# A two-layer sequence model on one core: dt's softplus moved out of PSUM, its sum to GpSimd, and four edits of order

## The chip, the core and the metric

One NeuronCore of a Trainium2 chip runs the whole program. It has TensorE (PE, matmul), VectorE (DVE), ScalarE (ACT), GpSimd (POOL) and the queue of SyncE (SP) that issues most transfers. The metric is the device time of one execution in microseconds; the time before is the median of three executions.

## What is computed

The input x is 4 x 1024 tokens of 256 values, all in float32. The first layer is a state-space block, the second a mixture of experts:

```python
# layer 1, on n = layernorm(x)
xc, z  = split(n @ W_in.T)                       # 256 + 256 columns
xs     = silu(conv3(xc, conv_w))                 # along the tokens
dt_param, Bp, Cp = split(xs @ W_x.T)             # 64, 16, 16
dt     = softplus(dt_param @ W_dt.T + b_dt) + 1e-5
s_t    = exp(-exp(A_log) * dt_t) * s_(t-1) + Bp_t * dt_t * xs_t   # 16 states a channel
y      = (Cp @ W_C.T) * sum_over_states(s) + D_param * xs
x      = x + layernorm((y @ W_out.T) * silu(z))
# layer 2, on n = layernorm(x): 8 experts, 2 for each token, and a shared one
out    = sum over the token's 2 experts e of weight_e * (gelu(n @ W1[e] + b1[e]) @ W2[e] + b2[e])
out   += gelu(n @ sW1 + sb1) @ sW2 + sb2
x      = x + layernorm(out)
```

## The kernel before

**Tiles.** The 4096 tokens are cut into NC = 8 chunks of TC = 512. Layer 1 holds the channels on the 128 partitions in two halves (c = 0, 1) and the chunk's 512 tokens along the free axis. Each chunk needs 32 scans: k = 0 to 31 counts 16 states times two halves. For each state TensorE spreads one row of Bp over the partitions (`spread`, L1007), VectorE multiplies it by u = dt * xs (`mult`, L1274) and runs the recurrence (`scan`, L1299), ScalarE makes the factors A = exp(nea * dt) (`decay`, L1587), and GpSimd adds the finished state to the sum of states (`scan` on its side, L1717, tile Ssum).

**The order.** Nothing schedules at run time. `timetable()` runs once in Python and writes one list of steps, PLAN; every engine walks that list and issues its own part of each step, so an engine's instructions stand in the list's order and a waiting instruction holds up all that stand behind it on that engine. The clock of the list is the scan: `main(i)` yields once per scan k of chunk i, and beside it run generators that are advanced by a share of their steps at each k:

- `prep(i + 1)`: layer norm, transpose (`xT`, L948), x and z projections (`xc`, L962; `z`, L976), convolution, silu, `dbc`, and dt of the next chunk, advanced by `prepare(k)` between FIRST_PREP = -3 and LAST_PREP = 27.
- `post(i - 1)`: of the chunk before, the product with C (`cmat`, L1012; `ymul`, L1305), the out projection, the gate, two layer norms (`stats` and `normal` of kinds 2 and 3, with `residual`, L1725, between), the stores, the transpose `nT` (L1035) and the gate's logits.
- `route(r)`: in three rounds, the top 2 and the tables that sort tokens by expert (`table`, L1736, GpSimd's indirect transfers).
- `pairs()`: groups of 256 tokens through the second layer, two at a time. A group is 8 `up` matmul pairs in four steps (L1077 for the shared expert, L1088 for a routed one), one `gelu` over both groups' hidden values (L1643, with a load of the activation table ahead of it and behind it), four `down` steps (L1121), and for a routed group a `gather` (L1747) ahead and a `scatter` (L1767) behind, both indirect transfers issued by GpSimd. In the last chunks `calls` = 58 steps of it are taken in each chunk.

Steps that fall due later stand in `agenda` and are written out by `tick()`, which also asks `fetch()` for the next gather and weights.

**PSUM.** Of 8 banks, 3 belong to the scan and NGEN = 5 go round among all other steps. A step in TAKING takes a bank, one in GIVING gives it back. `room()` lets a group's matmul take one only while at most NGEN - 3 are open.

**dt.** For chunks 1 to 7 ScalarE writes relu(p + b) from the bank into dts (L1563) and |p + b| back into the bank (L1567), then exp(-|.|) and ln(1 + .) in place in the bank (L1572, L1575). VectorE adds the bank, 1e-5 and dts into dts (`dt_sum`, L1262), which gives the bank back. GpSimd multiplies dts by xs into us (L926).

**The end.** When the last scan is done, all 8 banks are free for groups, `direct()` runs the remaining groups back to back, and `finishing()` does the last layer norm and the result chunk by chunk.

## Time and profile before

| | |
|---|---|
| runs of the kernel before | 1190.28, 1192.75, 1194.93 us; median 1192.75 |
| the profiled execution's own time | 1200.83 us |
| its span, first to last instruction | 1199.0 us |
| mean granted TensorE clock | 0.898 |
| busy, share of the span | PE 85%, PEld 68%, DVE 55%, ACT 54%, POOL 57% |
| chain that ended last, by engine | PE 54%, POOL 18%, issue 11%, DVE 8%, ACT 7%, DMA 1% |
| largest lines of that chain | L1121 22%, L1088 12%, L1717 9%, L1077 7%, L1100 6%, L1299 4%, L1736 3% |
| L1717 GpSimd's adds | x240, 303.1 us busy, 1287 ns mean |
| L1299 VectorE's scans | 148.3 + 141.2 us (x120 each) |
| L1747, L1767 gathers and scatters | x71 each, 70.2 and 112.5 us on POOL |

A view by stretches is read as follows: the preamble ends and the first scan starts at 35.5 us; the eight chunks' first scans start at 35.5, 97.4, 162.5, 232.5, 311.5, 389.6, 473.8 and 562.5 us; the last scan ends at about 654 us; from about 744 us to 1189 us TensorE runs groups alone; the last 10 us hold the final layer norm of the last 256 tokens and the last stores. Idle time of an engine is put to the instruction in front of which it passed, with what released it.

### The profile page before, as it was taken

The page shows a single profiled execution, that of the slowest core. Times are in us where ns is not written, and L with a number is a line of the kernel's source. Part 1 is how long each engine was busy: PE and PEld are TensorE (multiplying, and loading weights), DVE is VectorE, ACT ScalarE, POOL GpSimd, SP SyncE. Part 2 cuts the span into 40 slices and gives each one's busy share as a digit, 9 for nine tenths or more (in the row PEclk, how much of TensorE's full clock was granted, in tenths as well). Part 3 has the DMA queues.
Part 4 walks back from the last instruction along what each step waited for, and adds up shares of the span by engine and source line. Part 5 has one row for each costly group of instructions (what it writes and reads, how often), then busy time and mean ns, then how long its engine had stood idle before and what let it go on. Part 6 is the DMA issues. An engine that isn't in the chain of part 4 may idle for free.

```text
span 1199.0 us, 15407 instructions
## 1 busy us (share of the span) xinstructions
PE 1020.7 (85%) x4654; PEld 820.6 (68%) x4654; DVE 662.3 (55%) x1158; ACT 642.4 (54%) x1238; POOL 684.7 (57%) x666
## 2 busy tenths in 40 slices
PE   5437497878978879988949897999999999999996
PEld 3213175656656557766737775889999999998885
DVE  6899999998988898878955350010011000010333
ACT  5776869778587686886652531233333333333342
POOL 0687967769489997799774446432433333322211
PEclk9667587877968898999979997999999999999998
DMA  8210010202002016144463582598999988863511
GB/s 286 63 36 1 35 36 18 71 1 88 1 18 71 1 53 212 37 137 111 104 169 109 163 272 52 146 297 249 349 313 309 303 278 269 275 180 62 175 63 53
DMA packets 141635, 163.91 MB, mean 137 GB/s; under 512 B 26344, under 2 KB 126976, under 8 KB 141536
## 3 DMA queue, kind: packets, MB, share of 16 engines
q1 hardware_dynamic: 125872, 144.20, 37.1%
q0 software_dynamic: 15680, 18.72, 8.0%
q8 instruction: 37, 0.61, 0.2%
q14 instruction: 46, 0.38, 0.1%
HBM read 136.57 MB, written 26.74 MB: 136 GB/s over the span
## 4 chain that ended last, share of the span: by engine, by line
PE 54%; POOL 18%; issue 11%; DVE 8%; ACT 7%; DMA 1%; SPq 0%; DVEq 0%; POOLq 0%; ACTq 0%
PE psum L1121 22%; PE psum L1088 12%; POOL Ssum L1717 9%; PE psum L1077 7%; PE psum L1100 6%; DVE S L1299 4%; POOL list_d L1736 3%; ACT A L1587 2%; DVE psum L1274 1%; PE psum L962 1%; PE psum L1043 1%; PE psum L1064 1%; POOL scale L1661 1%; POOL gb L1725 1%; POOL acc_d L1767 1%
## 5 line engine op out<-in xcount | busy, mean ns | idle before, releaser
L1717 POOL TENSOR_TENSOR Ssum<-Ssum,S 128x512 f32<-128x512 f32 x240 | 303.1, 1287 | 73.4 <-DVE S L1299 72.5
L1121 PE MATMUL psum<-w,hT 128*128 128x256 f32 x1136 | 255.0, 382 | 8.5 <-issue 7.0
L1767 POOL DMA_INDIRECT acc_d<-y,ID x71 | 112.5, 1584 | 243.0 <-DMA acc_d<-y,ID 121.4
L1121 PEld LDWEIGHTS psum<-w,hT 128*128 128x128 f32 x1136 | 215.1, 192 | 38.3 <-issue 7.8
L1587 ACT ACTIVATE A<-dts,nea 128x512 f32<-128x512 f32 x256 | 175.2, 718 | 54.2 <-DVE S L1299 40.8
L1088 PE MATMUL psum<-XT,w 128*128 128x256 f32 x800 | 188.3, 390 | 15.2 <-issue 10.9
L1088 PEld LDWEIGHTS psum<-XT,w 128*128 128x128 f32 x800 | 154.4, 195 | 46.6 <-issue 17.7
L1274 DVE TENSOR_TENSOR psum<-us,psum 128x512 f32<-128x512 f32 x256 | 163.2, 683 | 35.6 <-PE psum L1007 35.4
L1299 DVE TENSOR_TENSOR_SCAN S<-A,carry,psum 128x512 f32<-128x512 f32 x120 | 148.3, 1266 | 0.2 <-issue 0.2
L1299 DVE TENSOR_TENSOR_SCAN S<-A,psum 128x512 f32<-128x512 f32 x120 | 141.2, 1205 | 3.3 <-POOL Ssum L1717 2.9
L1626 ACT ACTIVATE hT<-psum,bb 128x256 f32<-128x256 f32 x200 | 83.7, 471 | 105.0 <-PE psum L1088 71.7
L1077 PE MATMUL psum<-nT,s 128*128 128x256 f32 x512 | 134.3, 419 | 0.2 <-DVE nb L1312 0.2
L1431 DVE TENSOR_TENSOR psum<-bb,psum 128x256 f32<-128x256 f32 x71 | 26.9, 423 | 192.8 <-PE psum L1121 180.8
L1637 ACT ACTIVATE y<-psum,ID 128x256 f32<-128x256 f32 x71 | 29.8, 471 | 187.8 <-DVE psum L1431 180.5
L1121 PE MATMUL psum<-s,hT 128*128 128x256 f32 x512 | 127.5, 403 | 2.9 <-ACT hT L1643 2.9
L1421 DVE COPY XT<-psum 128x512 f32<-128x512 f32 x35 | 24.2, 691 | 188.3 <-PE psum L1064 155.5
L1077 PEld LDWEIGHTS psum<-nT,s 128*128 128x128 f32 x512 | 109.2, 214 | 21.7 <-issue 2.3
L1121 PEld LDWEIGHTS psum<-s,hT 128*128 128x128 f32 x512 | 104.3, 205 | 28.6 <-issue 12.9
L1007 PE MATMUL psum<-bst,SEL 96*128 96x512 bf16 x128 | 57.8, 453 | 71.8 <-DVE S L1299 66.5
L1747 POOL DMA_INDIRECT G<-xn_d,ID x71 | 70.2, 989 | 32.3 <-issue 18.5
L1007 PEld LDWEIGHTS psum<-bst,SEL 96*128 96x128 bf16 x128 | 14.2, 111 | 100.8 <-DVE S L1299 82.9
L1626 ACT ACTIVATE hT<-psum,sb1t 128x256 f32<-128x256 f32 x128 | 53.1, 469 | 50.4 <-PE psum L1077 50.2
(165 smaller groups left out, 1277.1 us busy)
## 6 DMA issues: line engine op xcount, KB each, us to landing
w<-W SPq DMA_DIRECT2D x92, 1024.0 KB
bb<-b SPq DMA_DIRECT2D x46, 128.0 KB
xnb<-x SPq DMA_DIRECT2D x16, 256.0 KB, 3.0
Xr<-x SPq DMA_DIRECT2D x16, 256.0 KB
x_d<-gb SPq DMA_DIRECT2D x8, 512.0 KB
xn_d<-nb SPq DMA_DIRECT2D x8, 512.0 KB
X<-x_d SPq DMA_DIRECT2D x16, 256.0 KB, 8.8
ACC<-acc_d SPq DMA_DIRECT2D x16, 256.0 KB, 5.4
```

What stands on the lines that cost most here:

```text
L1007: eng.matmul(BB[m % 2], SEL[:, n:n + 1].to_broadcast([96, 128]), bst[i % 2], start=True, stop=True).then_inc(spread, 1)
L1077: t = eng.matmul(ps[:, 256 * f:256 * f + 256], s1[:, k, 128 * (2 * u + f):128 * (2 * u + f) + 128], nT[i % 3][:, k, 256 * q:256 * q + 256] ...
L1088: t = eng.matmul(ps[:, 256 * f:256 * f + 256], w1[SLOT["w1", unit]][:, k, 128 * (2 * u + f):128 * (2 * u + f) + 128], XT[at % 2][:, k, :], ...
L1100: t = eng.matmul(ps[:, 128 * f:128 * f + 128], w1[SLOT["w1", unit]][:, k, 128 * (f0 + f):128 * (f0 + f) + 128], XT[at % 2][:, k, 128 * hal ...
L1121: t = eng.matmul(bank(g)[:, 256 * k:256 * k + 256], hT[n % 2][:, f, 128 * k:128 * k + 128], w[:, f, :], start=f == 0, stop=f == 7)
L1274: eng.tensor_tensor(bb if c else UB, us[i % 2][:, c, :], bb, ALU.mult).then_inc(mult, 1)
L1299: eng.tensor_tensor_scan(to, A[m % NA], BB[(m // 2) % 2] if c else UB, first, ALU.mult, ALU.add).then_inc(scan, 1)
L1587: eng.activation(A[m % NA], dts[i % 2][:, c, :], ACT.Exp, scale=nea[:, c, n:n + 1]).then_inc(decay, 1)
L1626: t = eng.activation(hT[n % 2][:, 2 * u + f, :], ps[:, 256 * f:256 * f + 256], fn, bias=bias[:, 2 * u + f:2 * u + f + 1])
L1717: eng.tensor_tensor(to, to, of, ALU.add).then_inc(nsum, 1)
L1747: eng.indirect_dma_start(G[n % 2][:, k, :], None, xn_d[0:TC * ROUND_END[r], :], bass.IndirectOffsetOnAxis(ap=ID[:, col, 0:1].bitcast(u32), ...
L1767: eng.indirect_dma_start(acc_d, bass.IndirectOffsetOnAxis(ap=ID[:, col, 1:2].bitcast(u32), axis=0), y[n % NY][:, k, :], None, compute_op=A ...
```

## The change

Six things are altered; the first is the title's, the others are of order.

1. **dt.** For all chunks |p + b| is written to us in SBUF, exp and ln work there in place, and the bank is given back at `dt_out`. For chunks 1 to 7 ScalarE adds 1e-5 in one more pass for each half (Identity with a bias), and GpSimd adds dts and us into dts; VectorE keeps the sum for chunk 0 only. `room()` now lets a group take a bank while at most NGEN - 2 are open.
2. **quiet.** While the two late layer norms of a chunk are under way, new gathers and due scatters are held back; `stats` of kind 2 and of kind 3 stand one scan later.
3. **The first chunk.** prep(1) is advanced from k = 0 on rather than from a start of -3.
4. **calls** goes from 58 to 54.
5. **The last chunk's final norm** is done in two halves (`last_stats`, `last_normal`, `last_result`).
6. **keep_busy.** TensorE multiplies zeros, 11 matmuls of 128x256 ahead of the first transposes and 3 ahead of the first projection.

```diff
     def tick():
 
         now[0] += 1
-        due = [row for at, row in agenda if at <= now[0]]
-        agenda[:] = [(at, row) for at, row in agenda if at > now[0]]
+        held = [item for item in agenda if item[0] > now[0] or quiet[0] and item[1][0] == "scatter"]
+        due = [row for at, row in agenda if (at, row) not in held]
+        agenda[:] = held
...
-        while len(open_uses) > room_for[0] - (2 if past[0] else 3):
+        while len(open_uses) > room_for[0] - 2:
             yield
...
         say("gated", i, 0, w0)
+        quiet[0] = not late
         yield
         say("gated", i, 1, w1)
-        yield from normalised(2, i, late)
+        yield
+        say("stats", 2, i)
+        quiet[0] = False
+        yield
+        yield
+        say("normal", 2, i, late)
+        quiet[0] = not late
+        yield
+        yield
         say("residual", i, late)
+        quiet[0] = False
         yield
         if not late:
             yield
             yield
+            quiet[0] = True
+            yield
             yield
         say("store_x1", i, late)
-        yield from normalised(3, i, late)
+        say("stats", 3, i)
+        quiet[0] = False
+        yield
+        yield
+        say("normal", 3, i, late)
+        yield
+        yield
...
-        if n < min(listed[0], turned[0] + 2):
+        if n < min(listed[0], turned[0] + 2) and not quiet[0]:
             say("gather", n)
...
-    def prepare(k):
+    def prepare(i, k):
 
         nonlocal done_prep
-        want = min(n_prep, -(-n_prep * (k + 1 - FIRST_PREP) // (LAST_PREP + 1 - FIRST_PREP)))
+        first = FIRST_PREP if i else 0
+        want = min(n_prep, -(-n_prep * (k + 1 - first) // (LAST_PREP + 1 - first)))
...
-                calls = 58 if listed[0] else 26
+                calls = 54 if listed[0] else 26
...
+    say("last_stats", 0)
+    yield
+    say("normal", 4, NC - 2, False)
+    say("result", NC - 2)
+    say("last_normal", 0)
+    say("last_result", 0)
+    yield
+    say("last_stats", 1)
+    say("last_normal", 1)
+    say("last_result", 1)
...
+            def keep_busy(ps, of, n):
+
+
+                for _ in range(n):
+                    eng.matmul(ps[:, 0:256], of[:, 0:128], of, start=True, stop=True)
...
-                    eng.activation(ps, ps, ACT.Abs, bias=bdt[:, c:c + 1]).then_inc(dt_out, 1)
+
+                    eng.activation(us[i % 2][:, c, :], ps, ACT.Abs, bias=bdt[:, c:c + 1]).then_inc(dt_out, 1)
                 elif step == "softplus":
-                    i, *gs = a
-                    for c in range(2):
+                    i, = a
+                    first = 6 * i - 2 if i else 0
+                    halves = [us[i % 2][:, c, :] for c in range(2)]
+                    for c, h in enumerate(halves):
                         eng.wait_ge(dt_out, 4 * i + 2 * c if i else c + 1)
-                        eng.activation(bank(gs[c]), bank(gs[c]), ACT.Exp, scale=-1.0).then_inc(softp, 1)
-                    for c in range(2):
-                        eng.wait_ge(softp, 4 * i + c + 1)
-                        eng.activation(bank(gs[c]), bank(gs[c]), ACT.Ln, bias=1.0).then_inc(softp, 1)
+                        eng.activation(h, h, ACT.Exp, scale=-1.0).then_inc(softp, 1)
+                    for c, h in enumerate(halves):
+                        eng.wait_ge(softp, first + c + 1)
+                        eng.activation(h, h, ACT.Ln, bias=1.0).then_inc(softp, 1)
+                    if i:
+                        for c, h in enumerate(halves):
+                            eng.wait_ge(softp, first + c + 3)
+                            eng.activation(h, h, ACT.Identity, bias=eps).then_inc(softp, 1)
...
+                elif step == "dt_sum":
+                    i, c = a
+                    if i:
+                        eng.wait_ge(softp, 6 * i + 3 + c)
+                        eng.tensor_tensor(dts[i % 2][:, c, :], dts[i % 2][:, c, :], us[i % 2][:, c, :], ALU.add).then_inc(dt_done, 1)
```

**TensorE, the start of the scans in chunk 0** (bst, SEL: spread; C, xnb: transposes of chunk 1; xnT, wxz: its projections). Before:

```order
L1007 MATMUL psum<-bst_131,SEL 128x512 x2
L948 MATMUL psum<-C,xnb 128x128 x8
L1007 MATMUL psum<-bst_131,SEL 128x512
L962 MATMUL psum<-xnT,wxz 128x512 x2
L1007 MATMUL psum<-bst_131,SEL 128x512
```

With the change:

```order
L1050 MATMUL psum<-bst_131,SEL 128x512 x3
L989 MATMUL psum<-C,xnb 128x128 x8
L1050 MATMUL psum<-bst_131,SEL 128x512
L1005 MATMUL psum<-xnT,wxz 128x512 x2
L1050 MATMUL psum<-bst_131,SEL 128x512
```

One more spread, that of state 2, stands ahead of the eight transposes; from there on each spread has moved one piece of chunk 1's preparation forward.

**ScalarE in chunk 2, around the gelu of the first pair of groups** (hT: hidden values; A: decays; edge, xs, zs: silu of the next chunk; gb: the layer norm of kind 2). Before:

```order
L1643 ACTIVATE hT_102<-hT_102 128x2048
L1463 ACT_TABLE_LOAD
L1587 ACTIVATE A_134<-dts_123,nea 128x512
L1527 ACTIVATE xs_122<-edge,xs_122,cw 128x1
L1530 ACT_TABLE_LOAD
L1530 ACTIVATE xs_122<-xs_122 128x512
L1527 ACTIVATE xs_122<-edge,xs_122,cw 128x1
L1530 ACTIVATE xs_122<-xs_122 128x512
L1534 ACTIVATE zs_128<-zs_128 128x1024
L1463 ACT_TABLE_LOAD
L1587 ACTIVATE A_135<-dts_123,nea 128x512
L1486 ACTIVATE gb<-gb,scale 128x256 x4
```

With the change:

```order
L1725 ACT_TABLE_LOAD
L1725 ACTIVATE hT_101<-hT_101 128x2048
L1725 ACTIVATE hT_102<-hT_102 128x2048
L1533 ACT_TABLE_LOAD
L1669 ACTIVATE A_139<-dts_123,nea 128x512
L1586 ACTIVATE xs_122<-psum,cw 128x512
L1586 ACTIVATE us_126<-psum,cw 128x512
L1586 ACTIVATE dts_124<-psum,cw 128x512
L1669 ACTIVATE A_140<-dts_123,nea 128x512
L1592 COPY zs_128<-psum 128x512
L1669 ACTIVATE A_141<-dts_123,nea 128x512
L1669 ACTIVATE A_142<-dts_123,nea 128x512
```

The gelu stood directly ahead of the silu and its two table loads, with the norm behind them; now it stands among the copies of the convolution's taps (xs, us, dts from psum), ten rows ahead of the silu. The same is found in chunks 3, 4 and 5.

**GpSimd in chunk 7, from the residual (gb) to the statistics of kind 3 (scale from mv30)**. Before:

```order
L1725 TENSOR_TENSOR gb_148<-Xr0_117,gb_148 128x512
L1725 TENSOR_TENSOR gb_148<-Xr1_118,gb_148 128x512
L1717 TENSOR_TENSOR Ssum11_146<-Ssum11_146,S_147 128x512
L1717 TENSOR_TENSOR Ssum10_145<-Ssum10_145,S_147 128x512
L1767 DMA acc_d<-y0_103,ID_69 4224x256 x2
L1717 TENSOR_TENSOR Ssum11_146<-Ssum11_146,S_147 128x512
L1717 TENSOR_TENSOR Ssum10_145<-Ssum10_145,S_147 128x512
L1767 DMA acc_d<-y1_104,ID_69 4224x256 x2
L1747 DMA G1_106<-xn_d,ID_69 128x256 x2
L1658 TENSOR_SCALAR scale_93<-mv30_89 128x4
L1659 TENSOR_SCALAR scale_93<-mv30_89 128x4
```

With the change:

```order
L1825 TENSOR_TENSOR gb_148<-Xr0_117,gb_148 128x512
L1825 TENSOR_TENSOR gb_148<-Xr1_118,gb_148 128x512
L1817 TENSOR_TENSOR Ssum11_146<-Ssum11_146,S_147 128x512
L1867 DMA acc_d<-y0_103,ID_69 4224x256 x2
L1867 DMA acc_d<-y1_104,ID_69 4224x256 x2
L1817 TENSOR_TENSOR Ssum10_145<-Ssum10_145,S_147 128x512
L1847 DMA G1_106<-xn_d,ID_69 128x256 x2
L1817 TENSOR_TENSOR Ssum11_146<-Ssum11_146,S_147 128x512
L1817 TENSOR_TENSOR Ssum10_145<-Ssum10_145,S_147 128x512
L1817 TENSOR_TENSOR Ssum11_146<-Ssum11_146,S_147 128x512
L1740 TENSOR_SCALAR scale_93<-mv30_89 128x4
L1741 TENSOR_SCALAR scale_93<-mv30_89 128x4
```

Both scatters (acc_d) and the gather (G1) still stand between the residual and the scale of kind 3, the two scatters now one behind the other; the adds (Ssum) that followed them stand behind, three of them right ahead of the scale.

## Rows read from the trace of the kernel before

**Rows 1.** Windows view: us; busy PE, PEld, DVE, ACT, POOL; PEclk; DMA share; GB/s
```profile
389.60:473.80 84.20, 68.83 (x282) 51.58 (x280) 73.02 (x120) 60.84 (x106) 75.70 (x72) 0.88 0.31 95
473.80:562.50 88.70, 79.40 (x345) 60.78 (x344) 72.79 (x119) 67.67 (x112) 73.86 (x76) 0.98 0.27 78
562.50:654.00 91.50, 72.40 (x326) 58.95 (x326) 67.64 (x96) 47.73 (x81) 62.67 (x58) 0.91 0.48 127
...
744.00:1189.00 445.00, 442.11 (x2403) 397.88 (x2403) 60.13 (x151) 150.37 (x409) 143.54 (x128) 0.99 0.73 222
```

**Rows 2.** Waits view, whole span: total us, times, longest us
```profile
DVE psum L1274 <- PE psum L1007: 35.4, 12, 13.0
...
POOL gb L1725 <- ACT gb L1486: 18.7, 4, 7.2
...
DVE stats L1181 <- POOL gb L1725: 11.6, 8, 3.5
...
DVE psum L1305 <- POOL Ssum L1717: 8.6, 3, 4.5
```

**Rows 3.** Timeline, preamble: start us, us, engine, line, [idle before <- releaser]
```profile
8.58 1.97 PE L948 MATMUL psum<-C,xnb 128*128 128x128 f32 x8 [8.58 <-ACT xnb L1486]
...
12.07 5.99 PE L962 MATMUL psum<-xnT,wxz 128*128 128x512 f32 x8 [1.22 <-ACT xnT L1497]
...
18.82 0.75 DVE L1232 SCALAR_TENSOR_TENSOR xs<-psum,cw,xs 128x511 f32<-128x511 f32 x1 [0.42 <-ACT xs L1510]
```

**Rows 4.** Timeline, first chunk, VectorE
```profile
44.95 1.29 DVE L1274 TENSOR_TENSOR psum<-us,psum 128x512 f32<-128x512 f32 x2 [3.69 <-PE psum L1007]
```

**Rows 5.** Tile and line views: count, ns min/median/max, first and last start us
```profile
L1262 DVE SCALAR_TENSOR_TENSOR dts<-psum,dts x16: 661/681/691, 30.0 to 547.0; 128x512 f32<-128x512 f32 x16
...
L926 POOL TENSOR_TENSOR us<-dts,xs x14: 1257/1264/1271, 88.5 to 552.8; 128x512 f32<-128x512 f32 x14
...
L1572 ACT ACTIVATE psum<-psum x16: 536/572/579, 28.4 to 539.3; 128x512 f32<-128x512 f32 x16
...
L1530 ACT ACTIVATE xs<-xs x16: 629/630/631, 19.5 to 502.7; 128x512 f32<-128x512 f32 x16
```

**Rows 6.** Timeline, chunk 2: ScalarE's gelu, VectorE's second statistics
```profile
185.83 3.71 ACT L1643 ACTIVATE hT<-hT 128x2048 f32<-128x2048 f32 x2
...
200.07 0.75 DVE L1181 BATCH_NORM_STATS2 stats<-gb 128x6 f32<-128x256 f32 x2 [2.38 <-POOL gb L1725]
```

**Rows 7.** Timeline, end of chunk 4: dt's sum, u on GpSimd, the next mult
```profile
378.52 1.28 DVE L1262 SCALAR_TENSOR_TENSOR dts<-psum,dts 128x512 f32<-128x512 f32 x2
...
386.44 2.49 POOL L926 TENSOR_TENSOR us<-dts,xs 128x512 f32<-128x512 f32 x2
...
388.39 1.29 DVE L1274 TENSOR_TENSOR psum<-us,psum 128x512 f32<-128x512 f32 x2 [0.62 <-PE psum L1007]
```

**Rows 8.** Timeline, chunk 6, TensorE and VectorE
```profile
527.66 2.71 PE L1121 MATMUL psum<-s,hT 128*128 128x256 f32 x8 [2.92 <-ACT hT L1643]
...
535.89 1.29 DVE L1274 TENSOR_TENSOR psum<-us,psum 128x512 f32<-128x512 f32 x2 [5.76 <-PE psum L1007]
```

**Rows 9.** Timeline, chunk 7: GpSimd, ScalarE and VectorE
```profile
610.87 1.55 POOL L1767 DMA_INDIRECT acc_d<-y,ID  x1 [2.42 <-DMA acc_d<-y,ID]
...
618.86 2.08 ACT L1486 ACTIVATE nb<-gb,scale 128x256 f32<-128x256 f32 x4 [9.65 <-POOL scale L1663]
...
629.19 1.29 DVE L1274 TENSOR_TENSOR psum<-us,psum 128x512 f32<-128x512 f32 x2 [13.04 <-PE psum L1007]
...
637.79 1.29 DVE L1274 TENSOR_TENSOR psum<-us,psum 128x512 f32<-128x512 f32 x2 [4.96 <-PE psum L1007]
```

**Rows 10.** Timeline, the end of the span, GpSimd and VectorE
```profile
1189.50 1.40 DVE L1181 BATCH_NORM_STATS2 stats<-ACC 128x6 f32<-128x256 f32 x4
...
1191.39 0.58 POOL L1658 TENSOR_SCALAR scale<-mv 128x4 f32<-128x4 f32 x1 [18.89 <-DVE mv L1187]
...
1194.54 1.28 DVE L1458 TENSOR_TENSOR X<-X,ACC 128x512 f32<-128x512 f32 x2
```

More of the change, by code:

```diff
@@ L88, in timetable @@
     now, room_for, listed = [0], [NGEN], [0]
+    quiet = [False]
     def say(*row):
@@ L207, in prep @@
             say("stats_x", 6)
-        for c, t in enumerate((t0, t1)):
-            say("dt_sum", i, c, t)
+        for c in range(2):
+            say("dt_sum", i, c)
             say("u", i, c)
@@ L553, in timetable @@
         chunk, whole = divmod(done, 2)
-        if n >= 2 and n % 2 and (whole or chunk < LATE or ("s", chunk, 1) in summed):
+        if n >= 2 and n % 2 and (whole or chunk < LATE or ("s", chunk, int(chunk < NC - 1)) in summed):
             part(final, 1)
@@ L563, in finishing @@
 def finishing(say):
-    for i in range(NC):
+    for i in range(NC - 1):
         say("stats", 4, i)
@@ L941, in _ @@
                     ps = take(g)
+                    if i == c == 0:
+                        eng.wait_ge(zeroed, 1)
+                        keep_busy(ps, G[0][:, 0, :], 11)
                     if c == 0:
@@ L959, in _ @@
                         eng.wait_ge(got_cw, 32)
+                    if i == c == 0:
+                        keep_busy(ps, G[0][:, 0, :], 3)
                     eng.wait_ge(xT_out, 2 * i + 2)
@@ L1200, in _ @@
                         read = edge_mv, 2
+                elif step == "last_stats":
+                    q, = a
+                    n = 2 * NC - 2 + q
+                    wait_whole(eng, NTH["s", NC - 1, q])
+                    eng.wait_ge(*read)
+                    for j in (2 * q, 2 * q + 1):
+                        i = eng.bn_stats(stats[:, j, :], of(4, NC - 1, j))
+                    i.then_inc(statd4, 1)
+                    eng.wait_ge(statd4, 2 * q + 1)
+                    if q == 0:
+                        eng.wait_ge(nmd[4], NC - 2)
+                    for j in (2 * q, 2 * q + 1):
+                        i = eng.bn_aggr(mv[4][(NC - 1) % 2][:, j, :], stats[:, j, :])
+                    i.then_inc(statd4, 1)
+                    read = statd4, 2 * q + 2
+                elif step == "last_normal":
+                    q, = a
+                    j = 2 * q + 1
+                    eng.wait_ge(nmd4, q + 1)
+                    eng.tensor_scalar(into(4, NC - 1, j), of(4, NC - 1, j), rs[4][(NC - 1) % 2][:, j:j + 1],
+                                      nm[4][(NC - 1) % 2][:, j:j + 1], ALU.mult, ALU.add).then_inc(normv[4], 1)
+                elif step == "last_result":
+                    q, = a
+                    n = 2 * NC - 2 + q
+                    eng.wait_ge(norma[4], 4 * (NC - 1) + q + 1)
+                    eng.wait_ge(normv[4], q + 1)
+                    eng.wait_ge(got_l[NC - 1], 32)
+                    eng.tensor_tensor(X1[n], X1[n], ACC[n], ALU.add).then_inc(resd, 1)
                 elif step == "stats_x":
@@ L1491, in _ @@
                         eng.preload_act_table_set("silu_and_others")
+                elif step == "last_normal":
+                    q, = a
+                    of, n = ACC[2 * NC - 2 + q][:, 0, :], (NC - 1) % 2
+                    eng.wait_ge(nmd4, q + 1)
+                    eng.activation(of, of, ACT.Identity, bias=nm[4][n][:, 2 * q:2 * q + 1],
+                                   scale=rs[4][n][:, 2 * q:2 * q + 1]).then_inc(norma[4], 1)
                 elif step == "xT_out":
@@ L1889, in _ @@
                         eng.dma_start(rows8(out[i // 2])[:, 2 * (n % 4):2 * (n % 4) + 2, :], X1[n]).then_inc(st_out[n % 4], 16)
+                elif step == "last_result":
+                    q, = a
+                    n = 2 * NC - 2 + q
+                    eng.wait_ge(resd, n + 1)
+                    eng.dma_start(rows8(out[NB - 1])[:, 2 * (n % 4):2 * (n % 4) + 2, :], X1[n]).then_inc(st_out[n % 4], 16)
             for k in range(4):
```

44 lines of the change are left out of this document (27 added, 17 removed).

## The prediction

> **What bounds the kernel now.** I first read the windows by stretch [rows 1]. From 744 us to 1189 us TensorE is busy 442.1 of 445.0 us: whatever is left when the scans end is worked off at a fixed pace, and nothing can be won there except work taken out of it. The order of the changed kernel takes none out: up to the last scan both plans hold 68 `up` and 64 `down` steps and 8 transposed groups. So the time moves by what the stretch of the scans, the preamble and the last ten microseconds lose, and by that alone.
>
> In the chunks VectorE is the busiest engine at first. Chunk 5 has GpSimd at 75.7 of 84.2 us against VectorE's 73.0, not counting what it loses between its own indirect transfers, so it is all but full; in chunks 6 and 7 no engine is full (TensorE 79.4 of 88.7, then 72.4 of 91.5), so these are chunks of waits [rows 1]. The waits view says which [rows 2]: VectorE stood 35.4 us for spreads, 12 times, the longest 13.0; 11.6 us for the residual by GpSimd, which itself stood 18.7 us for ScalarE's norm; and 8.6 us for the last adds of the states.
>
> **The change part by part**, against the profiled execution of 1200.8 us.
>
> *Preamble.* The first projections take 5.99 us for 8 records, most at the lower of TensorE's two clocks, and ScalarE's copy of the second ends 0.42 us after VectorE is free for it [rows 3]. VectorE is otherwise dense there, so warm matmuls can bring 0.5 us. Against it: 22 records of zeros stand ahead of the transposes. At the price of the slow projections (0.75 us a record of 512 columns, so 0.37 for 256) they take 8.2 us, and the last three matmuls, 6 records, 2.2 us, where TensorE had 8.58 us and then 1.22 us free [rows 3]. Bounds: 3 us lost, 1 us won; I take 0.5 won, since that gap and the faster projections behind it pay for the three.
>
> *First chunk.* The spread of state 2 stands behind the transposes of chunk 1, which wait for their input, and keeps VectorE for 3.69 us [rows 4]. It now stands ahead of them, and each later one has one piece of preparation fewer ahead. VectorE does one pair of scans more by the same time, 3.4 us (mult 1.29, the pair of scans 2.3, overlaps taken off). The two smaller waits behind it stay in part. Bounds 2 and 5.7.
>
> *dt's sum.* VectorE loses 2 x 0.68 us, 1.3 with the overlap, in each of chunks 0 to 6. GpSimd gains two adds at the price of its product u, 2 x 1.26 = 2.5 us [rows 5]. ScalarE gains two passes of 0.63 (the in-place silu in SBUF), 1.3 us. Exp and ln in SBUF rather than PSUM are four passes; in place in PSUM one took 0.57, the silu in SBUF 0.63 [rows 5], so 0.2 us more. ScalarE was busy 60.8 and 67.7 us in chunks 5 and 6 [rows 1] and has no queue that reaches the next chunk, so I charge it nothing; were that cover gone, it would cost 1.5 us a chunk.
>
> The Trainium skill says the same of the direction ("ScalarE: Activation LUTs", Step-by-step: what each stage is for): a write to PSUM is faster than one to SBUF. It speaks against this change; these rows put it at some 0.06 us a pass, and the sum is the same with or without it.
>
> Where GpSimd has room (chunks 0 to 3) VectorE's 1.3 us count in full: 5.2 us. In chunk 4 GpSimd reached u 7.9 us after VectorE had made dt (386.4 against 378.5), and VectorE then stood up to 4.5 us for the last add [rows 2, 7]. There the 2.5 us count, not the 1.3. The same holds for chunk 5.
>
> *Banks and the earlier gelu.* In chunk 2 the gelu (3.71 us and two table loads) stood ahead of silu and norm, the residual came behind the norm, and VectorE stood 2.38 us for its first half [rows 6]. Now it is ten rows earlier on ScalarE and the silu no longer stacks on it. Statistics of kind 3 also come one scan later. That removes nearly all of the 11.6 us [rows 2], but only where GpSimd does not bind: the eight waits lie in chunks 2 to 5, 2.9 us a chunk, and I count chunks 2 and 3, 5.8 us. In chunks 4 and 5 GpSimd's own waits for the norm go, some 5 us for both (18.7 in all, less the longest of 7.2 and one near it [rows 2]), less twice 2.5 for dt: nothing won. What is late next on ScalarE are the tap copies of the next chunk at scans 4 and 5; they have until scan 9, where the silu stands, so I cost them at nothing.
>
> *Holding back gathers and scatters* moves GpSimd's own work behind the norm's steps by one to three scans. Before chunk 5 there is none to hold, and later the group that needs a gather is two groups away, so I cost it at nothing; without that cover a transposed group would wait for it.
>
> *Chunk 6.* TensorE waited 2.92 us for the gelu (dt's second matmul and the spread stood behind it), and VectorE 5.76 us for that spread [rows 8]. The gelu comes one scan earlier, GpSimd has 2.5 us more, and four more `up` steps (6.9 us of TensorE) fall into this chunk, taken from the next. Bounds: 4 lost, 7 won; I take 2 won, near neither, because the extra matmuls eat most of the wait removed.
>
> *Chunk 7.* GpSimd waited for the first scatter's landing before it could issue the second (2.42 us), so the scale of kind 3 came late, ScalarE's norm waited 9.65 us, the gelu of two groups stood behind that norm, and TensorE's transposes and `down` steps held the spreads: 13.04 + 4.96 us of VectorE [rows 9]. In the new order both scatters and the gather still stand ahead of that scale, so GpSimd is as late as it was. But the gelu stands ahead of the norm now, so its 3.7 us and loads no longer come behind, and four `up` steps are gone from the chunk. Of 18 us I take 8 off; bounds 2 and 18.
>
> *The end.* Behind the last matmul stand a 0.69 us sum, statistics of four tiles, the scale on GpSimd, two norms and two results. Halved, the statistics save 0.7 of 1.40 and the results 0.6 of 1.28; aggregation and norm save 0.5 more by the same share. GpSimd's first step took 0.58 us against 0.24 elsewhere while VectorE added chunk 6's results [rows 10]; those now stand ahead of the last half, which saves 0.3 more on it and as much on the next step. 2.4 us.
>
> The Trainium skill has the reason ("SBUF — State Buffer", Who interferes with whom): a VectorE instruction with two SBUF inputs keeps GpSimd's reads out. The 0.58 us agree.
>
> **Sum:** 0.5 (preamble) + 3.4 (first chunk) + 5.2 (dt) + 5.8 (norm) + 2 + 8 (chunks 6, 7) + 2.4 (end) = 27.3 us. The profiled execution stood 8.1 us above the median of its runs; I take the same 27.3 off the median: 1192.75 - 27.3 = 1165.4.
>
> **The rivals.**
> 1. *GpSimd becomes the bound.* Its 2.5 us are paid in chunks 4 to 6, held-back scatters land on it in a heap, and chunk 7 keeps its 13 us wait. For: it is full in chunk 5, and the order of chunk 7. Against: 18.7 us of its waits are for the very norm that comes earlier. Gains in chunks 6 and 7 fall from 10 to 2 and chunks 4 and 5 cost 4: 27 - 8 - 4 = 15 won. 1178, from 1173 to 1184.
> 2. *The waits of chunks 6 and 7 go altogether.* They come from one queue that is late; once ScalarE is no longer stacked the lateness may not build. 7 + 18 instead of 10: 42 won, 1150.
> 3. *Nothing measurable, moved waits.* The gelu collides with the tap copies, the convolution comes late, and each chunk gives back at its `dbc` what it won. Left are the preamble, first chunk and end, 6 us, less GpSimd's price of 2.5: 1189.
> 4. *Slower: dt comes late at each boundary.* The decays of the next chunk now wait for GpSimd, in order behind its adds. At the end of chunk 4 GpSimd lagged 7.9 us; with its sums and u 13 us, where the next chunk's first mult came 9.9 us behind dt [rows 7]. That boundary would cost 3 us. From a lag of some 10 us at every boundary it decides: 7 boundaries at 5 us are 35, which is 8 more than the rest wins: 1200. Against: dt was last made at 547.0 [rows 5] and chunk 7's first scan came at 562.5, 15 us behind.
>
> **How the numbers follow.** A measurement of this kernel tells about 0.5%, 6 us, from no change. My forecast (20 to 36 us won) 0.56; rival 1 0.19; rival 2 0.13; rival 3 0.06; rival 4 0.06. Predicted 1165. The range leaves out rivals 3 and 4 and the ends of 1 and 2: 1151 to 1181. Faster 0.88, same 0.06, slower 0.06.
>
> **What would show it.** The first scans of chunk 2, 3 and 4 come earlier by some 6, 10 and 14 us than before; VectorE's waits for the residual are gone; u starts on GpSimd later behind VectorE's place than before, by 1.3 us; between 744 us and the end of the matmuls TensorE is as dense and as long. VectorE's waits for spreads fall from 35 us to about 20, the largest still in chunk 7. From the last matmul to the last instruction it takes 7.7 us rather than 10. I would be wrong in the step on chunk 7 if the longest wait is gone or whole, in the step on dt if ScalarE's decays stand for GpSimd's sum, and in the whole if the stretch of groups has grown by what the scans lost.

## The result and the profile after

| | before | changed |
|---|---|---|
| median of the runs | 1193.8 us (1190.28 to 1194.93, 4 runs) | 1205.49 us (1202.76 to 1206.2, 4 runs) |
| ratio, 95% interval | 1 | 1.0099 (1.0071 to 1.0126) |
| profiled execution: span, granted clock | 1199.0 us, 0.898 | 1203.6 us, 0.904 |
| last scan ends | 653.9 us | 655.1 us |
| last matmul ends | 1188.86 us | 1195.12 us |
| last matmul to end of the span | 10.1 us | 8.5 us |

The change costs about 12 us where I had forecast 27 won; the same kernel, run again on another chip (e13 below), gave a ratio of 1.0116. The two spans differ by only 4.6 us, since the profiled execution of before stood 8 us above its median; against the experiments below these 8 us lie behind the last scan.

First, the windows view of the changed kernel, a row for each of chunks 5, 6 and 7 and then the stretch of groups in four pieces (columns as in [rows 1]):

```profile
382.50:471.10 88.60, 65.45 (x282) 49.88 (x280) 71.69 (x118) 67.64 (x121) 77.79 (x74) 0.87 0.30 90
471.10:562.10 91.00, 80.73 (x362) 63.89 (x361) 71.58 (x118) 67.69 (x112) 72.93 (x74) 0.96 0.28 76
...
562.10:655.10 93.00, 74.22 (x315) 60.09 (x314) 68.19 (x97) 50.59 (x85) 67.57 (x62) 0.88 0.46 133
655.10:700.00 44.90, 39.96 (x166) 32.37 (x165) 13.08 (x35) 18.99 (x31) 21.47 (x23) 0.90 0.51 140
700.00:760.00 60.00, 59.11 (x301) 52.43 (x300) 17.46 (x70) 18.59 (x42) 34.36 (x33) 1.00 0.55 155
760.00:870.00 110.00, 93.38 (x525) 83.42 (x524) 10.16 (x21) 28.68 (x85) 38.63 (x32) 0.94 0.85 251
870.00:1195.10 325.10, 325.10 (x1769) 292.70 (x1767) 51.01 (x132) 113.72 (x306) 100.61 (x96) 1.00 0.71 220
```

The first scans of the chunks came at 35.2, 92.4, 160.7, 229.8, 305.8, 382.5, 471.1 and 562.1 us, where before they came at 35.5, 97.4, 162.5, 232.5, 311.5, 389.6, 473.8 and 562.5. So 5 us are won by chunk 1 and 7 in all by chunk 5; chunks 5 to 7 give everything back. I had forecast the first scans of chunks 2, 3 and 4 to come 6, 10 and 14 us earlier; they came 1.8, 2.7 and 5.7 us earlier. Then TensorE, which I had taken for fully fed, stands 16.6 of the 110 us from 760 us on. Before, from 744 us to the end, it stood 2.9 us [rows 1].

Waits view of the changed kernel (total, times, longest), for [rows 2]:

```profile
DVE psum L1348 <- PE psum L1050: 48.8, 21, 11.1
...
ACT A L1669 <- POOL dts L1794: 21.5, 10, 5.4
...
DVE psum L1379 <- PE psum L1055: 18.0, 5, 7.2
```

VectorE's 11.6 us for the residual are gone, as the change says. But its waits for spreads have grown from 35.4 to 48.8 us (I had forecast about 20), its wait for the matmul of C (`cmat`, L1055) from 2.6 to 18.0, and ScalarE stands 21.5 us for GpSimd's sum of dt, where before it stood 6.0 us for VectorE's. The end of chunk 4 shows how these hang together (timeline; ScalarE, GpSimd, TensorE, VectorE), at the place of [rows 7]:

```profile
373.15 0.19 ACT L1680 COPY lg<-psum 128x32 f32<-128x32 f32 x1 [3.24 <-PE psum L1086]
...
377.59 0.72 ACT L1669 ACTIVATE A<-dts,nea 128x512 f32<-128x512 f32 x1 [4.26 <-POOL dts L1794]
380.17 2.56 ACT L1669 ACTIVATE A<-dts,nea 128x512 f32<-128x512 f32 x4 [1.86 <-POOL dts L1794]
...
383.96 2.06 ACT L1556 ACTIVATE xnb<-xnb,scale 128x256 f32<-128x256 f32 x4
```
```profile
373.85 2.49 POOL L1817 TENSOR_TENSOR Ssum<-Ssum,S 128x512 f32<-128x512 f32 x2
376.30 1.26 POOL L1794 TENSOR_TENSOR dts<-dts,us 128x512 f32<-128x512 f32 x1
```
```profile
386.17 0.63 PE L989 MATMUL psum<-C,xnb 128*128 128x128 f32 x4 [3.20 <-ACT xnb L1556]
...
388.68 1.12 PE L1055 MATMUL psum<-dbc,wc 16*128 16x512 f32 x2
```
```profile
389.91 0.70 DVE L1379 TENSOR_TENSOR psum<-Ssum,psum 128x512 f32<-128x512 f32 x1 [4.98 <-PE psum L1055]
```

The operands of the sum were ready at 367.2 us (end of the Identity pass). GpSimd, in order behind its adds of the states, began it at 376.3. On ScalarE the decay of the next chunk (A) waits for it, and everything else stands behind that decay: the groups' copies and the norm of kind 1 (xnb). Behind that norm stand TensorE's transposes, behind these the spread and C's matmul, and VectorE loses 4.98 us.

And the stretch of groups, its fetches (SyncE) and TensorE's gap:

```profile
719.32 3.53 SPq L1966 DMA_DIRECT2D bb<-b  x1
763.05 0.38 SPq L1944 DMA_DIRECT2D ID<-list_d  x1
...
774.27 0.39 SPq L1962 DMA_DIRECT2D w<-W  x1
```
```profile
773.93 1.09 PE L1107 MATMUL psum<-C,G 128*128 128x128 f32 x4 [5.07 <-DMA G<-xn_d,ID]
783.26 9.10 PE L1131 MATMUL psum<-XT,w 128*128 128x256 f32 x32 [8.24 <-DMA bb<-b]
```

The last round's lists are read back from 763.05 us on (755.56 before). Behind them, in order on SyncE, the next weights are fetched at 774.27 (766.57 before), and TensorE stands for them until 783.26.

### The profile page after: what moved, and what is told of

Its sections match the earlier page's. It is cut to its first block, busy times and chain, and to the rows that moved or that the text cites. A ratio compares the mean times of both kernels' runs of the same rounds, so it can differ in the third digit from the quotient of the medians.

```text
span 1203.6 us, 15481 instructions
## 1 busy us (share of the span) xinstructions
PE 1006.0 (84%) x4682; PEld 817.5 (68%) x4682; DVE 654.3 (54%) x1145; ACT 648.9 (54%) x1252; POOL 703.6 (58%) x684
## 4 chain that ended last, share of the span: by engine, by line
PE 45%; POOL 17%; ACT 12%; issue 11%; DVE 5%; SPq 4%; DMA 3%; POOLq 0%; DVEq 0%; ACTq 0%
PE psum L1164 19%; PE psum L1131 8%; POOL Ssum L1817 8%; PE psum L1120 7%; PE psum L1143 5%; ACT A L1669 3%; POOL list_d L1836 3%; DVE S L1373 2%; ACT hT L1725 2%; DMA acc_d<-y,ID 2%; DMA bb<-b 1%; SPq L1942 1%; PE psum L1066 1%; ACT hT L1708 1%; PE psum L1086 1%
## 5 line engine op out<-in xcount | busy, mean ns | idle before, releaser
L1164 PE MATMUL psum<-w,hT 128*128 128x256 f32 x1136 | 257.9, 385 | 8.2 <-issue 6.5
L1131 PE MATMUL psum<-XT,w 128*128 128x256 f32 x800 | 184.4, 388 | 14.0 <-DMA bb<-b 8.2
L1348 DVE TENSOR_TENSOR psum<-us,psum 128x512 f32<-128x512 f32 x256 | 163.2, 683 | 49.1 <-PE psum L1050 48.8
L1120 PE MATMUL psum<-nT,s 128*128 128x256 f32 x512 | 126.5, 401 | 0.0
L1164 PE MATMUL psum<-s,hT 128*128 128x256 f32 x512 | 118.2, 383 | 1.2 <-ACT hT L1725 1.2
L1120 PEld LDWEIGHTS psum<-nT,s 128*128 128x128 f32 x512 | 103.5, 204 | 21.9 <-issue 5.0
L1164 PEld LDWEIGHTS psum<-s,hT 128*128 128x128 f32 x512 | 98.6, 193 | 21.4 <-issue 7.8
```

Of the source, the lines that this page charges most:

```text
L1120: t = eng.matmul(ps[:, 256 * f:256 * f + 256], s1[:, k, 128 * (2 * u + f):128 * (2 * u + f) + 128], nT[i % 3][:, k, 256 * q:256 * q + 256] ...
L1131: t = eng.matmul(ps[:, 256 * f:256 * f + 256], w1[SLOT["w1", unit]][:, k, 128 * (2 * u + f):128 * (2 * u + f) + 128], XT[at % 2][:, k, :], ...
L1164: t = eng.matmul(bank(g)[:, 256 * k:256 * k + 256], hT[n % 2][:, f, 128 * k:128 * k + 128], w[:, f, :], start=f == 0, stop=f == 7)
L1348: eng.tensor_tensor(bb if c else UB, us[i % 2][:, c, :], bb, ALU.mult).then_inc(mult, 1)
```

## The experiments

Four theories. **A**: the loss is the last routing round alone, late behind late logits. **B**: it is GpSimd's sum of dt; B1 by its place in GpSimd's order, B2 by its 2.5 us of work. **C** (formed after the first eight runs): the stretch behind the scans depends on where the last chunk's closing steps stand among the group steps (the `up` and `down` steps). "The stretch" is from the end of the last scan to the end of the last matmul. Each run was timed beside the kernel before; a ratio is to that, on its own chip. Edits are against the changed kernel and cut to what matters.

**e1: closing steps twice as fast behind the last scan.**
```diff
     for _ in beside:
         tick()
-        part(last, 1)
+        part(last, 2)
```


> The changed kernel with one edit: behind the last scan the last chunk's closing steps advance two, not one, per matmul step of the groups, so that its logits stand 10 group steps behind the last scan instead of 22 (15 in the kernel before). Theory A (the loss is the last routing round, which comes late behind logits moved off beat, so that TensorE has no group ready between 760 and 800 us): the gap there, about 14 us, goes, and the time is 1193 +-3, some 12 us less than the changed kernel's 1205.5. Theory B (the loss is GpSimd's sum of dt, which ScalarE's decays wait for in the chunks; the gap is only where the lateness shows): nothing is won or at most 4 us, 1201 to 1206.

1.0100 (1.0077 to 1.0123). The gap at 760 us shrank to 7.0 us, but TensorE now stood 10.8 us between 655 and 700 for the closing steps themselves; the stretch came to 536.5 us. Theory A in this form fell.

**e2: the sum on VectorE.**
```diff
-                    if i == 0:
-                        eng.wait_ge(softp, 3 + c)
-                        eng.scalar_tensor_tensor(dts[0][:, c, :], us[0][:, c, :], 1e-5, dts[0][:, c, :],
+                    eng.wait_ge(softp, 4 * i + 3 + c)
+                    eng.scalar_tensor_tensor(dts[i % 2][:, c, :], us[i % 2][:, c, :], 1e-5, dts[i % 2][:, c, :],
...
 ScalarE's Identity pass and GpSimd's sum are taken out
```


> The changed kernel with dt's sum made by VectorE from SBUF in all chunks, without ScalarE's Identity pass; order of steps untouched. Theory B: ScalarE's 21.5 us of waits for GpSimd's sum go, and with them a part of VectorE's 48.8 us for spreads; 5 to 10 us won, 1196 to 1200. Theory A: the order and its late logits are the same, the gap at 760 us stays at 12 us or more, and VectorE pays 1.3 us a chunk again: 1203 to 1210.

1.0033 (1.0019 to 1.0047), 1193.91 us: by the ratios 8 us won against the changed kernel. The last scan ended at 644.9 instead of 655.1. B stands, though the stretch stayed at 539.9 us.

**e3: all but dt; e4: dt, banks and end alone.**
```diff
 e3: dt's softplus, sum, banks and room as in the kernel before
 e4: calls 58, no holding back, no zero matmuls, statistics and first chunk as before
```


> The kernel before (dt's softplus in PSUM, sum on VectorE, banks held) with all the other parts of the change: gathers held back and statistics one scan later, first chunk's preparation, 54 calls, halved end, zero matmuls. Its logits stand 13 group steps behind the last scan, and 4 group steps fewer (6.9 us) lie beside the scans. Theory B (dt is what costs): faster than the kernel before by the preamble, first chunk and end, 3 to 8 us, 1186 to 1191. Theory A: the same range, since its logits are not late; so this run tells of the order edits' worth alone. If it comes at 1200 or more, the order edits carry the loss and both theories fall.

> The kernel before with dt's softplus in SBUF and GpSimd's sum, the banks freed, and the halved end; no other edit of the order (58 calls, no holding back, statistics as before, no zero matmuls). Logits 16 group steps behind the last scan. Theory A: dt is harmless and its logits are not late, 1185 to 1192. Theory B: dt is what costs, 1197 to 1205.

e3: 1.0022 (1.0013 to 1.0032), so it misses my 1186 to 1191; e4: 1.0200 (1.0181 to 1.0219), 1214.19 us, worse than B had asked (1197 to 1205). In e3 the last scan ends at 636.2, with 128 group steps done instead of 132, yet the stretch behind is 547.2 us. Taking off 6.9 us for the four steps leaves 540.3. In e4, with 136 steps done, 532.9 + 6.9 = 539.8. Four orders of the closing steps (the changed kernel's, e1, e3, e4) gave 536.5 to 540.3; the next runs showed 527.4 and 527.5 for that of before, and this led to theory C.

**e5: the sums two scans earlier on GpSimd.**
```diff
         say("softplus", i)
         yield
         yield
+        if i:
+            for c in range(2):
+                say("dt_sum", i, c)
         yield
         say("low_out", i)
...
         for c in range(2):
-            say("dt_sum", i, c)
+            if not i:
+                say("dt_sum", i, c)
```


> The changed kernel with one edit: GpSimd's two sums of dt stand two scans (3.8 us of VectorE) earlier in its order, ahead of the copy of C's rows and of u, which stay. Theory B1 (the loss is the lateness of the sums: ScalarE's decay of the next chunk stands for them, up to 5.4 us, and behind that decay stand its gelus and its norm of kind 1, for which TensorE's transposes and the spreads behind them wait): 8 to 14 us won, 1189 to 1195, and ScalarE's 21.5 us of waits for the sums fall under 5. Theory B2 (the loss is GpSimd's 2.5 us a chunk of work, wherever it stands): at most 3 us won, 1199 to 1203.

1.0078 (1.0057 to 1.0100), 1199.45 us: inside B2's range (1199 to 1203) and outside B1's, and by its interval not clear of the changed kernel's 1.0099. ScalarE's waits for the sum fell to 3.6 us, as B1 had asked, and VectorE's for C's matmul from 18.0 to 10.5. But VectorE still stood 13.9 us for GpSimd's `Ssum` (10.5 in the changed kernel) and 50.8 for spreads (48.8); the last scan came 4.1 us earlier, where e2 had brought 10.2.

**e6, e7, e8: dt's parts on the plan of before.**
```diff
 e6, e7, e8: all other parts of the change taken back
 e6: SBUF softplus, Identity, sum on GpSimd; banks held until the sum
 e7: SBUF softplus, sum on VectorE; banks held until the sum
 e8: e7 with banks given back at dt_out, room - 2
```


> The kernel before, its plan row for row, with dt's softplus in SBUF, the Identity pass and the sum on GpSimd, the banks held until the sum as before. If the sum on GpSimd alone carries what the run with dt, banks and halved end showed (23 us): 1208 to 1214. If the freed banks' reordering carries most of it: 1193 to 1198.

> The kernel before, its plan row for row, with dt's softplus in SBUF and the sum on VectorE from there (no Identity pass, nothing on GpSimd). Prices exp and ln in SBUF, my 0.2 us a chunk: 1189 to 1193. If ScalarE's longer passes or VectorE's SBUF reads cost something on the path: 1194 or more.

> As the run with SBUF alone (plan of before otherwise, sum on VectorE), with the two banks given back at dt's copies and the room widened by one, so that gelus stand earlier and 4 more matmul steps lie beside the scans. My prediction's step (residual waits go, 5.8 us and the waits of chunks 6 and 7): 1180 to 1186. If the earlier gelu only moves the waits: 1189 to 1193. If it harms (spreads behind more matmuls): 1195 or more.

e6: 1.0210 (1.0189 to 1.0231), 1215.51 us, just above my 1208 to 1214; e7: 1.0029 (1.0012 to 1.0045), 1194.61 us, at the edge of my "1194 or more"; e8: 1.0078 (1.0053 to 1.0103). The exchange from VectorE to GpSimd thus costs 1.8%, 21 us, in an otherwise equal plan: the last scan ends at 675.3 in e6 and at 654.5 in e7, and the stretches behind are equal, 527.4 and 527.5. In this and all other runs the exchange includes ScalarE's Identity pass, two of 0.72 us a chunk; no run prices that pass by itself. Waits view of e6:

```profile
ACT A L1661 <- POOL dts L1786: 29.0, 12, 6.7
...
PEld psum L1108 <- POOL dts L1786: 13.3, 5, 8.1
...
PE psum L1108 <- POOL dts L1786: 10.6, 3, 7.6
```

With the banks held, TensorE's `up` steps wait for GpSimd too. e8 is against my expectation. In its profile the last scan at 663.1 with four more steps done (6.9 us) is 1.6 us late, and the stretch has lost 13 (533.5 + 6.9 = 540.4). But the profiled execution was e8's slowest, 1208.50 us; by the medians e8 lies only 6.7 us above e7, and how these are shared is not shown.

**e9: the kernel before once more; e10, e11: the old places; e12: no sum.**
```diff
 e10: the changed kernel
-                calls = 54 if listed[0] else 26
+                calls = 52 if listed[0] else 26
     in post(), stats 2:
-        yield
+        if not late:
+            yield
 e11: e10 with e2's edit
 e12: GpSimd's dt_sum on [:, c, 0:1]
```


> The kernel before, unchanged, profiled once more, because the profiled execution of it that I read stood 8 us above its median. If the run with SBUF alone is a fair model of it: scans of the last chunk end at 652 to 655 us as in the first profile, and the last matmul ends at 1181 to 1183 rather than 1188.9, so that the stretch from the last scan to the last matmul is 528 us and not 535; the 8 us then lie between 700 and 760 us. Otherwise the 8 us lie elsewhere, in the chunks too.

> The changed kernel with 52 calls in place of 54 and, in the last chunk alone, the statistics of kind 2 at once as before. That puts the last chunk's closing steps behind the last scan as they were (cmat 0, logits 15, tables 24, lists 40 group steps; 132 steps beside the scans). Theory C (the stretch from last scan to last matmul is set by the place of these steps among the group steps: 528 us in the three profiles with the old places, 540 in every other order): this stretch is 527 to 530 us and the time 1190 to 1194. Without it (the stretch depends on what the chunks leave): 540, and 1201 to 1205.

> The same with dt's sum on VectorE from SBUF. Theory C and B together: the last scan ends near 645 us, the stretch is 528, and the time is 1180 to 1184, 8 us or so below the kernel before. If the two gains are not additive: 1188 to 1194.

> The changed kernel with GpSimd's two sums of dt a chunk shrunk to one element each (dt then lacks its logarithm, so the output is another), the Identity pass and all waits kept. What the 2.5 us of GpSimd work a chunk cost, apart from the sum's place behind GpSimd's adds. If the work costs (theory B2): 10 us or more won, 1188 to 1194. If its place does (B1): 1198 to 1202.

These four fell on a chip on which the kernel before took 1201.16 us. e10: 1.0054 (1.0036 to 1.0072); e11: 0.9973 (0.9957 to 0.9989); e12: 1.0052 (1.0035 to 1.0069). None of the stretches came at the 528 us expected: 537.3 in e9, 539.5 in e10, 537.6 in e11. Set beside e7, e9 shows where the 8 us of my first profile lie, since its last scan too ended at 653.3. Windows view of e9, and then of e7, the same order:

```profile
720.00:745.00 25.00, 15.11 (x44) 9.20 (x43) 0.99 (x2) 3.35 (x8) 16.58 (x16) 0.75 0.23 47
```
```profile
720.00:745.00 25.00, 25.00 (x122) 22.06 (x121) 3.23 (x8) 6.66 (x17) 19.21 (x20) 1.00 0.33 67
```

The profiled kernels with the old places (before, e9, e10, e11) lose 8 to 11 us between 700 and 760 on this chip and in the first profile; all other profiles lose at most 5.3 (e16), mostly 1 to 3. e12, with the changed kernel's places, loses 2.8 here. So on this chip C's sign did not come, and the ratios say little of it while that loss lies on top; C needed another chip. In e12 (which computes another result, since dt lacks its logarithm) the last scan ended at 655.6, as in the changed kernel, though ScalarE's waits for the sum had halved (10.4 us): without GpSimd's work but with the sum at its late place nothing is won there. That speaks against B2. The time of e5 speaks against B1 as the whole cause. Left are the two together, or the Identity pass, which both runs kept; how they share the loss is not shown.

**e13 to e16: the changed kernel, the old places, VectorE's sum, and old dt, on one chip.**
```diff
 e13: the changed kernel    e14: e10    e15: e11
 e16: e3 with calls = 58 and stats 2 of the last chunk at once
```


> The changed kernel itself, as a yardstick for the three kernels beside it on the same chip. Stretch from last scan to last matmul 540 us, no loss of TensorE between 720 and 745 us. Where the kernel before takes 1191: 1203. On a chip where it takes 1201: 1203 too if the loss between 720 and 745 us belongs to the old places alone.

> The same kernel as the run with 52 calls and the old places, now beside the changed kernel. Theory C: on a chip where the kernel before takes 1191 the stretch is 527 to 530 us and the time 1190 to 1195, 10 us under the changed kernel's; on one where it takes 1201, within 3 us of the changed kernel's. Without theory C: as the changed kernel on both.

> The same with dt's sum on VectorE from SBUF. Theories B and C: on a chip where the kernel before takes 1191, 1181 to 1187; on one where it takes 1201, 1197 as measured there.

> dt as before in every way (PSUM, VectorE, banks held), with all other parts of the change, 58 calls and the last chunk's statistics of kind 2 at once, which gives the old places of the closing steps and 132 steps beside the scans. The first chunk wins 4 us, the later ones up to 5, the end 2: on a chip where the kernel before takes 1191, 1180 to 1186. If the order edits are worth nothing beyond the end: 1189 to 1191.

| | ratio, 95% interval | median us | last scan | to last matmul |
|---|---|---|---|---|
| e13 | 1.0116 (1.0096 to 1.0137) | 1204.01 | 657.4 | 536.8 |
| e14 | 1.0074 (1.0049 to 1.0100) | 1198.68 | 656.2 | 528.4 |
| e15 | 0.9974 (0.9964 to 0.9984) | 1187.28 | 650.1 | 527.8 |
| e16 | 0.9925 (0.9909 to 0.9942) | 1181.24 | 641.9 | 526.7 |

Windows view of the same 110 us in e13 and in e14:

```profile
760.00:870.00 110.00, 95.38 (x533) 85.21 (x532) 10.16 (x21) 29.49 (x87) 39.53 (x32) 0.94 0.86 253
```
```profile
760.00:870.00 110.00, 103.88 (x574) 93.18 (x573) 10.76 (x22) 32.93 (x94) 41.74 (x34) 0.97 0.93 283
```

Theory C holds on this chip: with the old places the stretch is 8.4 us shorter in the profiles, from the same last scan within 1.2 us, and the lists are read back at 755.32 instead of 764.15. The median of e14 won 5 us, less than that, with a spread of 1194.95 to 1204.29; the profiled execution was the fastest. Two other pairs agree: from e2 to e15 the ratio goes from 1.0033 to 0.9974 and the stretch from 539.9 to 527.8, from e3 to e16 the ratio from 1.0022 to 0.9925 and the stretch (four steps taken off) from 540.3 to 526.7. e15 came at 1187.28, just above what B and C together asked (1181 to 1187). e16 beats both kernels: 9 us under the one before.

What makes the old places good is not simply that they are early. The kernels' plans have the last round's first lists 40 group steps behind the last scan before and 47 in the changed kernel, but 39 in e3 and 35 in e1, whose stretches are no shorter. TensorE stood 12.9 us (e3) and 10.8 us (e1) between 655 and 700 us there, against 4.1 in e16.

**e17, e18: e16 taken apart.**
```diff
 e17: e16 without holding back, statistics 2 and 3 as before
 e18: e16, its plan row for row, with e6's dt
```


> As e16, with gathers and scatters not held back and the statistics of kinds 2 and 3 where they stood before: left are the first chunk, the zero matmuls and the halved end. By my prediction holding back costs and brings nothing and the later statistics remove VectorE's 11.6 us for the residual only with the freed banks: within 3 us of e16, 1181 to 1184 where the kernel before takes 1190. If they carry the gain: 1185 to 1188, and the last scan ends near 650 us.

> As e16, its plan row for row (banks held until the sum), with dt's softplus in SBUF, the Identity pass and the sum on GpSimd. The same exchange cost 21 to 25 us on the plan of the kernel before. If its price is the wait of ScalarE's decays and of TensorE's groups for the sum: 15 to 25 us over e16, 1196 to 1206 where the kernel before takes 1190. If the order edits are what takes the sting out of it: under 10 us over e16.

e17: 0.9963 (0.9950 to 0.9975); e18: 1.0121 (1.0099 to 1.0144). Holding back and the later statistics are worth 4.5 us, against my "nothing" (last scan 648.8 against 641.9); first chunk, zero matmuls and end carry the other 4.4. From e16 to e18 the softplus in SBUF and the sum on GpSimd together cost 23 us (last scan 666.5 against 641.9), much as on the old plan, where the same two (e6 against the kernel before) cost 25. Windows view, the last chunk in e16:

```profile
558.60:641.90 83.30, 71.38 (x325) 58.17 (x325) 67.53 (x96) 47.63 (x80) 61.01 (x56) 0.94 0.50 139
```

## Why the prediction was wrong

Put together from the profiles, against an undisturbed execution of the kernel before (last scan 654, stretch 527.5 as in e7; of the kernel itself no such profile was taken): scans +1 to +3 us, stretch +9 to +13, end -1.7. That makes the 12 measured. Inside the scans -12 by the order edits (e16) meet +13 to +15 by dt and the freed banks.

- **"Whatever is left when the scans end is worked off at a fixed pace": wrong, and the largest error.** I compared the numbers of `up` and `down` steps at the last scan (68 and 64 in both) and not the order of the closing steps behind it. In the changed order the logits of chunk 7 stand 20 group steps behind the last scan instead of 14 (22 and 15 where a group's transposes are counted too, as in my expectations), the last round's tables 28 instead of 24, its lists 47 instead of 40. The row that I rested it on, 442.1 of 445 us, showed that the old order just sufficed, and not that any order would. I had named this sign ("if the stretch of groups has grown by what the scans lost") and given it no chance.
- **dt's sum: wrong in sign.** I had 5.2 us won in chunks 0 to 3, nothing in 4 and 5, and charged ScalarE nothing. VectorE's part is there, and so is GpSimd's size: the sum took 1.27 us, twice a chunk. But the exchange costs 21 us with banks held (e6 against e7), and 8 to 12 with banks freed, by three pairs of ratios: 1.0099 and 1.0033 (changed kernel, e2), 1.0054 and 0.9973 (e10, e11), 1.0074 and 0.9974 (e14, e15). Against rival 4 I had held that dt was made at 547.0 and the first scan came at 562.5, 15 us behind. That was the wrong reader. The first decay of chunk 5 started at 377.59, 4.9 us ahead of its scan, and what counts is what stands behind it on ScalarE.
- **Exp and ln in SBUF:** 0.62 us against 0.57 and 0.55 in PSUM, as I had taken it (0.06 a pass). That agrees with the Trainium skill ("ScalarE: Activation LUTs", Step-by-step: what each stage is for), by which ScalarE writes faster to PSUM than to SBUF, though here the reads moved with the writes. In e7 the scans end 0.7 us later than before; its ratio says 3 us, and where the rest of these lie is not shown. The Identity pass took 0.72, not 0.63.
- **Banks and the earlier gelu:** the mechanism was right and its worth wrong. The 11.6 us for the residual went, but not into the time. With GpSimd's sum the last scan comes 10 us earlier with freed banks (666.5 in e18, 656.2 in e14); the waits of TensorE's `up` steps for the sum (7.0 us of PE in e18) are gone in e14. With VectorE's sum freed banks brought no gain: 650.1 in e15 against 641.9 in e16, where plan and softplus differ as well.
- **Holding back and later statistics, "cost at nothing":** they win. In e16 chunk 7 takes 83.3 us, in e17 91.7, before 91.5. So 8 us are won in chunk 7, but by these edits and not by the gelu, and shown only with the banks held. With the banks freed chunk 7 took 88.9 us (e2) to 94.5 (e15); the changed kernel's takes 93.0 and keeps a wait of 11.10 us at 636.29.
- **Chunk 6, 2 us won:** it took 91.0 us instead of 88.7, so 2.3 lost, inside my bounds. Chunk 5, which I had at nothing, took 88.6 instead of 84.2.
- **Preamble and first chunk: right.** 0.3 us won by the first scan (0.5 forecast), 4.7 in chunk 0, where I had 3.4 (bounds 2 and 5.7) and 1.3 for dt. With the old dt (e17) chunk 0 takes 58.3 us instead of 61.9, so 3.6 belong to the order. The zero matmuls did what I took them for: the eight records of the projections took 3.70 us instead of 5.99 (3.70 in e3 and e13 too, 5.89 in e4 without the zeros). But I had called the 5.99 us "at the lower of TensorE's two clocks": the windows view has a granted clock of 1.00 from 12 to 18 us in both kernels, so that reading is not borne out, and why they were slow without the zeros is not shown.

```profile
11.53 3.70 PE L1005 MATMUL psum<-xnT,wxz 128*128 128x512 f32 x8
```

- **Chunk 1 gave 3.2 us back at once.** GpSimd's late sum carries this: with the sum earlier (e5) chunk 1 took 65.5 us instead of 68.3, with VectorE's (e2) 65.0. ScalarE's wait of 5.40 us for the sum at 85.98 us is not new in itself: before it stood 5.52 us for VectorE's sum at 87.81. New is a second wait of 1.84 us behind it, for the other half.
- **End: right, with less won than forecast.** 8.5 us from the last matmul to the end, 7.7 forecast, 10.1 before. GpSimd's first step took 0.58 us in the first half, beside VectorE's adds of chunk 6's result (1189.92 to 1191.18 us), and 0.23 in the last half, alone. That agrees with the Trainium skill ("SBUF — State Buffer", Who interferes with whom), by which a VectorE instruction with two inputs in SBUF contends with a GpSimd instruction that reads SBUF:

```profile
1190.10 0.58 POOL L1759 TENSOR_SCALAR scale<-mv 128x2 f32<-128x2 f32 x1 [11.33 <-DVE mv L1258]
...
1197.00 0.23 POOL L1759 TENSOR_SCALAR scale<-mv 128x2 f32<-128x2 f32 x1 [4.78 <-DVE mv L1258]
```

Of the rivals the fourth had the true mechanism inside the scans, at 0.06, and named the right boundary, the end of chunk 4. Its 5 us at each of seven boundaries did not come: ScalarE's waits for the sum at the ends of chunks 0 to 6 were 7.2, 2.5, 1.8, 3.1, 6.1, 0 and 0.7 us. That its 1200 lies nearest to the 1205 measured is luck, since 9 to 13 us of the loss lie in the stretch, which no rival had.

Left open: what property of the old places makes the stretch short; what the Identity pass costs by itself; why chunks 5 and 6 suffer most from the sum (in e18 chunk 5 is 10 us longer than in e16, 94.6 against 84.3); whether a sum on GpSimd between the places of the changed kernel and e5 would pay; and how the freed banks' order and calls of 52 share the 8 us between e15 and e16.

## What to carry to other kernels

When a step moves to another engine, look for its first reader and for what stands behind that reader in order; the slack to a later reader, here the scan, said nothing. A rate in a planner (here calls per chunk, or how many banks may be open) also sets the phase of every serial chain that runs beside the filler work, so compare the places of the last chain among the filler steps, and not only their number. An engine that is 99% busy in one order is a fact about that order.

## What was not expected of the hardware

In the kernels with the old places TensorE lost 9 to 11 us between 700 and 760 us in some executions: in the first profile of before, and on one chip in all three of these kernels. Elsewhere the same orders lost 1 to 5 us there. The timeline of e9 shows single matmuls 1.4 us apart with no releaser ("issue"); the granted clock was 1.00, 0.59 and 0.50 in the three pieces of 5 us from 730 us on (0.50 is the lower of its two levels, 1.2 GHz; it fell behind the idle time), and the DMA share was 0.01 to 0.02. GpSimd wrote list entries all the while, one each 1.26 us:

```profile
735.98 0.59 PE L1121 MATMUL psum<-w,hT 128*128 128x256 f32 x1 [1.02 <-issue]
737.38 0.58 PE L1121 MATMUL psum<-w,hT 128*128 128x256 f32 x1 [0.81 <-issue]
738.78 0.58 PE L1121 MATMUL psum<-w,hT 128*128 128x256 f32 x1 [0.82 <-issue]
```

The records are all there: both traces, e9's and e7's, hold 4654 matmul records. And TensorE was not alone. In e9 it began the transposes of a tile at 721.25 us (0.60 us long), and VectorE copied that tile only at 743.08, with no releaser on this core ("remote"); in e7 the transposes came at 724.20 and the copy at 724.89. By the copies at 814.22 and 805.63 the lag had shrunk to 8.6 us.

```profile
743.08 0.69 DVE L1421 COPY XT<-psum 128x512 f32<-128x512 f32 x1 [25.01 <-remote]
```

So more than TensorE was held up there. In the changed kernel GpSimd writes the same lists and TensorE stays busy. The cause stays open.
